# Opening block of a graph and expert kernel: who clears the sums, ScalarE's order, and the first increments

## What is computed

```python
x = x + _L0_gnn_ref(_layernorm(x, axis=-1), L0_gnn_W, src, dst, edge_weight)

def _L0_gnn_ref(X, W, edge_src, edge_dst, edge_vals):
    Z = jnp.matmul(X, W)                       # 1250 x 512 by 512 x 512
    msg = Z[edge_src] * edge_vals[:, None]     # 41250 edges, sorted by dst
    agg = jax.ops.segment_sum(msg, edge_dst, num_segments=X.shape[0])
    return jax.nn.relu(agg)
```

## Time and profile before

| | us |
|---|---|
| median of 3 runs | 1474.98 |
| lowest and highest | 1473.58, 1478.74 |
| the profiled execution | 1486.91 |
| its span | 1485.1 |
| TensorE busy in it | 1405.3 |
| VectorE busy in it | 750.1 |
| ScalarE busy in it | 464.1 |
| GpSimd busy in it | 225.5 |

### The profile page before, as it was taken

One profiled execution on the slowest core, in us unless ns is written; L12 is line 12 of the kernel. 1 busy time (PEld: TensorE's weight loads), 2 busy tenths in 40 slices (PEclk: granted clock), 3 DMA queues, 4 the chain that ended last, 5 costly groups with the idle time before them and its releaser, 6 DMA issues. The chain is left out here.

```text
span 1485.1 us, 24276 instructions
## 1 busy us (share of the span) xinstructions
PE 1405.3 (95%) x7939; PEld 904.7 (61%) x7940; DVE 750.1 (51%) x1591; ACT 464.1 (31%) x1153; POOL 225.5 (15%) x356
## 2 busy tenths in 40 slices
PE   8999999999999999999988999999899999889968
PEld 4688854455477777776556666666445555646632
DVE  7899956552278788875662222222250012544421
ACT  3599931111055555553021111111340011211111
POOL 1133310000000000000212222222420000012234
PEclk9999999999999999999998999999999999799988
DMA  5000000020000000001338999999420000823336
GB/s 153 29 0 0 0 0 0 0 85 0 28 2 2 1 2 1 2 1 48 113 72 271 322 332 322 328 323 324 138 60 0 0 0 0 301 53 128 127 95 171
DMA packets 94075, 142.38 MB, mean 96 GB/s; under 512 B 13301, under 2 KB 50571, under 8 KB 93879
## 3 DMA queue, kind: packets, MB, share of 16 engines
q1 hardware_dynamic: 69313, 97.52, 21.4%
q0 software_dynamic: 14976, 26.81, 6.5%
q10 hardware_dynamic: 9718, 17.12, 3.4%
HBM read 115.09 MB, written 26.29 MB: 95 GB/s over the span
## 5 line engine op out<-in xcount | busy, mean ns | idle before, releaser
L1240 PEld LDWEIGHTS ps<-b_r 128*128 128x128 f32 x1024 | 125.4, 193 | 34.3 <-issue 32.8
L1240 PE MATMUL ps<-b_r 128*128 128x78 f32 x1024 | 123.2, 274 | 1.1 <-DVE b_r L1302 1.1
L1249 PE MATMUL ps<-b_r 128*78 128x512 f32 x256 | 122.0, 600 | 0.0
L585 PE MATMUL ps<-b_r 125*125 125x160 f32 x660 | 118.3, 315 | 0.0
L500 ACT ACTIVATE b_r<-b_r 125x125 f32<-125x125 f32 x330 | 107.6, 389 | 9.2 <-DVE b_r L395 4.8
L1286 ACT ACTIVATE b_r<-ps,b_r 128x78 f32<-128x78 f32 x128 | 34.7, 323 | 230.5 <-PE ps L1240 226.7
L911 PEld LDWEIGHTS ps<-b_r 125*64 125x64 f32 x1600 | 85.3, 136 | 24.6 <-issue 22.8
L874 PE MATMUL ps<-b_r 64*125 64x417 f32 (+1 forms) x480 | 95.3, 529 | 1.4 <-DVE ps L1003 1.2
L911 PE MATMUL ps<-b_r 125*64 125x125 f32 x1600 | 94.7, 272 | 1.3 <-ACT b_r L939 1.3
L1144 POOL TENSOR_TENSOR b_x<-b_x,b_r 125x512 f32<-125x512 f32 x10 | 12.7, 1273 | 534.7 <-DVE b_r L1089 534.7
L1165 POOL DMA_INDIRECT b_r<-rows,b_ex_ids x88 | 85.7, 974 | 45.8 <-issue 40.7
(11 more groups left out here) (262 smaller groups left out, 2238.5 us busy)
## 6 DMA issues: line engine op xcount, KB each, us to landing
b_r<-L_ffn_w SPq DMA_DIRECT2D x128, 512.0 KB, 9.5
y<-b_r ACTq DMA_DIRECT2D x64, 156.0 KB
b_r<-L_ffn_W SPq DMA_DIRECT2D x2, 4096.0 KB, 20.5
y<-b_r ACTq DMA_DIRECT2D x24, 256.0 KB, 2.4
rows<-b_r SPq DMA_DIRECT2D x2, 2400.0 KB
b_x<-x SPq DMA_DIRECT2D x5, 480.0 KB
out<-b_x SPq DMA_DIRECT2D x10, 240.0 KB
y<-b_r SPq DMA_DIRECT2D x1, 2048.0 KB, 11.0
```

What stands on the lines that cost most here:

```text
L585: last = pe.matmul(T.ps[:P, 2 + b, 0:WC], T.weighted[:, b, j, :], T.cells[:, b, j, :], start=(j == 0), stop=(j == CJ - 1))
L1240: last = pe.matmul(T.ps[:, 2 + r % 2, f * CAP:(f + 1) * CAP], T.ew1[r % WS][:, k, f * 128:(f + 1) * 128], T.ex_t[:, r % 2, k, :], start=(k ...
L1249: last = pe.matmul(T.ps[:CAP, 4 + r % 2, :], T.eh[:, r % 2, f, :], T.ew2[r % WS][:, f, :], start=(f == 0), stop=(f == FK - 1))
```

## The change

Columns 3000 and up of the sums and all of the counts are cleared by GpSimd, in two memsets one behind the other. VectorE clears the first 3000 columns only. ScalarE takes the root of tile 6 ahead of product row 2, that of tile 7 behind the turned pair 2, and no longer loads the table of Copy. The increments of ScalarE and TensorE come at the head of their programs. Product 9 goes to bank 5 (which `turn_edges` used before it) and so waits for `columns_ready`, and TensorE's loop waits for nine copied rows, not ten.

```diff
-    BY_POOL, FIRST = 5000, 8000
+    BY_VECTOR = 3000
...
+    def z_bank(t):
+        return t % 2 if t < NT - 1 else 5
...
-            pool.memset(at[:, 0:BY_POOL], 0.0).then_inc(S.sums_cleared, 1)
+            pool.memset(at[:, BY_VECTOR:], 0.0).then_inc(S.sums_cleared, 1)
+            pool.memset(ct, 0.0).then_inc(S.sums_cleared, 1)
...
-            pool.wait_ge(S.sums_cleared, 4)
+            pool.wait_ge(S.sums_cleared, 3)
...
-            dve.memset(at[:, BY_POOL:FIRST], 0.0).then_inc(S.sums_cleared, 1)
+            dve.memset(at[:, 0:BY_VECTOR], 0.0).then_inc(S.sums_cleared, 1)
...
             prepare_edges(dve, link, T, S)
-            dve.memset(at[:, FIRST:], 0.0).then_inc(S.sums_cleared, 1)
-            dve.memset(ct, 0.0).then_inc(S.sums_cleared, 1)
             edge_columns(dve, link, T, S)
...
         def _(act):
+            act.sem_inc(S.weighted_ready, 2)
+            act.sem_inc(S.weights_copied, 2)
...
-                act.activation(T.rows_a[:, t, :], T.ps[:P, t % 2, :], ACT.Copy).then_inc(S.z_copied, 1)
+                act.activation(T.rows_a[:, t, :], T.ps[:P, z_bank(t), :], ACT.Copy).then_inc(S.z_copied, 1)
...
             product_row(1)
-            roots(3)
-            roots(4)
-            act.preload_act_table(ACT.Copy)
+            row_roots(act, T, S, 0, (6,))
             product_row(2)
             turned(2)
+            row_roots(act, T, S, 0, (7,))
+            roots(4)
             product_row(3)
...
-            act.sem_inc(S.weighted_ready, 2)
-            act.sem_inc(S.weights_copied, 2)
...
-                    last = pe.matmul(T.ps[:P, t % 2, :], T.feats[:, k, t * P:(t + 1) * P], T.w_a[:, k, :],
+                    last = pe.matmul(T.ps[:P, z_bank(t), :], T.feats[:, k, t * P:(t + 1) * P], T.w_a[:, k, :],
...
+            pe.sem_inc(S.counts_done, 2)
+            pe.sem_inc(S.products_done, 2)
             pe.wait_ge(S.ones_bf_ready, 1)
...
-            for t in (7, 8, 9):
-                product(t)
+            product(7)
+            product(8)
+            pe.wait_ge(S.columns_ready, 1)
+            product(9)
...
-            pe.sem_inc(S.counts_done, 2)
-            pe.sem_inc(S.products_done, 2)
-            pe.wait_ge(S.z_copied, NT)
-            pe.wait_ge(S.columns_ready, 1)
+            pe.wait_ge(S.z_copied, NT - 1)
```

More of the change, by code:

```diff
@@ L423, in _ @@
             dve.reg_mov(passed, 0)
-            dve.wait_ge(S.sums_cleared, 4)
+            dve.wait_ge(S.sums_cleared, 3)
             visits(dve, "dve", body, begin_pass, end_pass)
```

## The result

The changed kernel takes 1485.54 us at the median of 6 runs (1479.32 to 1490.11), the kernel before 1474.31 us at the median of 6 (1473.34 to 1478.74). The ratio is 1.0068 with a 95% interval of 1.0041 to 1.0096, so 6 to 14 us. The recorded ratio isn't quite that of the two medians, which differ by 11.2 us. The forecast was 1484.6 us.

What follows compares the result with a forecast made beforehand. It took the opening, TensorE busy nearly throughout, to set the loop's start. Terms +8.2 - 0.4 + 2.0 - 4.4 + 2.45 + 1.75 = +9.6 us on 1474.98 gave 1484.6 us; range 1472.5 to 1487.5.

Steps and rivals of the forecast that it cites:

- The clearing is not hidden: Opening: GpSimd's memsets block VectorE's `normalize`, so the first transposes come 8.2 us later; chance 0.66, hidden 0.23.
- Which tile waits: Opening, VectorE: tile 0's `normalize` waits for GpSimd's first memset until 11.25 us, tile 1's for the second, ending at 17.3.
- The rival in which both tiles slip in between the memsets: Opening: only the first memset holds VectorE up, first `turn` at about 12.3 us; +4.5 us, 1479.5 us; chance 0.08.
- The low clock at the restart: TensorE's first transposes start at the low clock after idling since 8.3 us: 2.0 us lost.
- ScalarE's order: At `product(4)`: row 2 copied straight behind product 2 removes the stand and the slow clock behind it, gaining 4.4 us.
- What is late next, `turn_edges`: TensorE waits at `turn_edges` for `prep_done`, delayed 0.8 us by tile 7's root: 2.45 us given back.
- The clock falls in that stand: At `turn_edges`: the array is empty some 2.3 us, so the clock falls, costing 1.75 us.
- The increments, row 9's copy, bank 5: At the loop's start: earlier increments gain 0, bounds 0 and 0.35 us; `product(9)` waiting for `columns_ready` costs nothing.

Runs made afterwards that it cites:

- the back-to-back pieces: Changed kernel with GpSimd's two memsets cut into 25 pieces (19 of 500, 6 of 1043 columns) without waits between them: 1486.40 us, ratio 1.0059.
- the pair of runs: Changed kernel with GpSimd's later clearing held until `prep_done`: roots of tiles 6 and 7 both early, 1473.74 us; roots in the change's order, 1473.66 us.
- the run with waiting pieces: Changed kernel with GpSimd's clearing in 25 pieces, each waiting for the end of the one before: 1476.87 us, ratio 0.9998.
- the two-input form: Changed kernel with the opening's `normalize` written as an operation with two SBUF inputs instead of `tensor_scalar`: 1478.08 us, ratio 1.0006.

## Why the prediction was right, and where it was off

**The clearing is not hidden: right, and shown.** The clearing alone makes 7.8 us (1.0053), all else of the change nothing that shows (1.0015), and a slower form of the same operation (0.75 us) runs unhindered beside the same memsets. The runs show that the two exclude each other; that a port is what they dispute is not shown by them. The Trainium skill's rule on the shared port pair ("SBUF — State Buffer", Who interferes with whom) agrees in what contends. It states the lock for a whole instruction. So it was where each piece waited for the one before (0.27 to 0.28 us behind the piece's end). Without such waits it lasted through rows of instructions: two memsets (8.96 us) and 25 (9.59 us).

**Which tile waits: wrong, the total right.** The step said that tile 0 gets in at 11.25 us between the two memsets, and that tile 1 then waits for the second, to 17.3 us. In fact tile 0 waited for both and tile 1 for none. The end came out the same, because both ways end behind the second memset: the first transposes were 8.26 us late, put at 8.2. So this number was in part luck, since it couldn't tell the two ways apart. The rival in which both tiles slip in between the memsets (4.5 us) is ruled out by tile 0's row, and by the back-to-back pieces.

**The low clock at the restart: 2.0 us put, 1.9 measured.** From turn 0 to turn 1 it took 26.32 - 17.51 = 8.81 us, against 16.57 - 9.25 = 7.32 us before, of which I take 0.4 us as the wait for the weights that vanished. Only the difference of the two terms is measured: 1.5 us, put at 1.6. The price isn't a fixed one: from turn 0 to turn 1 it took 8.53 us with the clearing alone and 9.71 us with the back-to-back pieces, behind an idle stretch of much the same length (8.45, 9.42 and here 9.86 us), as the clock stayed low for a shorter or longer time.

**ScalarE's order: right against the kernel before, but the clearing had taken part of the gain already.** There was no stand at product 4, and from turn 1 to turn 3 it took 40.05 - 26.32 = 13.73 us, against 34.74 - 16.57 = 18.17 us before: 4.4 us. The run without the table load shows most of them: 3.1 us up to row 9, with 0.75 us of stand left. With the clearing alone the same stretch took 15.73 us, with a stand of 1.73 us and no fall of the clock. So beside the new clearing the order was worth only 2.0 us, and `turn_edges` took that back.

**What is late next, `turn_edges`: right.** Tile 7's root delays it by 0.8 us (36.80 against 35.99 us in the pair of runs). The stand gave back 2.2 of the 4.4 us: `turn_edges` came at 46.60 us, 7.57 us behind before, where 9.75 - 4.4 = 5.35 us would be without it (9.75 us is the delay of turn 1). I had put 2.45 us.

**The clock falls in that stand: wrong in the profiled run.** This is the term that was mis-sized: 1.75 us put, 0 measured. The array was empty for 2.10 us, not 2.3, and the clock held, here and in three other runs with 2.10 us. It fell after 2.16 us in the run with waiting pieces and after 2.73 us with the two-input form, so the choice between the two was close either way. With this term the forecast for row 9 was +9.6 us. Measured was +7.67 us, and the terms as measured give 8.26 - 0.4 + 1.9 - 4.4 + 2.2 = 7.6 us.

**The increments, row 9's copy, bank 5: right for the changed kernel, but conditional.** The loop's first weighted product followed row 9's copy by 1.82 us instead of 2.01, so 0.2 us were gained, between the bounds of 0 and 0.35. VectorE had its two groups ready at 57 us and then waited 7.91 us for ScalarE. The wait of product 9 for `columns_ready` costs nothing only because VectorE's memsets are gone. With them back it stood 1.16 us.

**The size of the median.** The opening costs 7.5 us in the trace, the medians differ by 11.2 us, and the ratio says 10.0 us, with 6 to 14 us by its interval. The clearing alone is alike: its loop starts 7.1 us late in the trace, its medians differ by 10.0 us, and the ratio says 7.8 us (4.7 to 10.9). So the forecast of 1484.6 us came closer to 1485.54 us than its sum for the opening deserves, and that is luck. What lies between 7.5 and 11.2 us is within the scatter of the runs, and I can't say more on it.

## What to carry to other kernels

Work given to an idle engine is free only if it shares nothing with the busy one. Ask of every long GpSimd instruction which double-rate VectorE operations (`tensor_scalar` from SBUF to SBUF here) will be issued while it or its followers run, and who waits for them. Place such clearing where VectorE works in other forms, or let each of GpSimd's pieces wait for the one before. And when a stand is removed, work out first how early the next thing waited for can be there: here half of the 4.4 us went back to `turn_edges`.

## What the runs showed of the hardware

- GpSimd kept VectorE's `tensor_scalar` out over the ends of its instructions: 9.59 us through 25 back-to-back memsets. When each of the 25 waited for the one before, it took 0.66 us and ended 0.27 us behind the piece that it met. I had expected a handover at each end.
- A VectorE operation with two SBUF inputs ran at its own pace (0.75 us for 512 columns) beside a memset, while at the end of the edge loop a GpSimd addition took 0.83 us instead of 0.50 when it came 0.03 us behind a VectorE operation with two inputs. The addition reads SBUF, the memset doesn't; that this makes the difference is not shown.
- Around an empty array of 2.1 us the clock may hold or fall: it held after 2.10 us in four runs and fell after 2.16 us in one. With the fall, the stretch from `turn_edges` to turn 4 took 6.69 us with the waiting pieces and 8.10 us with the two-input form, instead of 5.03 us in the changed kernel, so a term of this kind can be off by 2 to 3 us when it is forecast from one trace.
